# One batch more of ctx and of y transposed by VectorE's 32x32 blocks instead of TensorE, with a few steps put in another order

## The reference, cut to what matters

```python
# x, ctx: (8, 256, 1024); Wq, Wk: (1024, 1024); all float32
text = layernorm(x)
Q = einsum('btx,dx->btd', text, Wq) + bq
K = einsum('bpx,dx->bpd', ctx, Wk) + bk
attn = softmax(einsum('btd,bpd->btp', Q, K) / 32)   # 256 x 256 for each batch
x1 = x + einsum('btp,bpd->btd', attn, ctx)
y = layernorm(x1)
w = 4-bit fields of qweight; wbin = where(w > 0, 1, -1)
weights = scales[g_idx] * (wbin - zeros[g_idx])     # 1024 x 1024
out = x1 + y @ weights + bias
```

## Time and profile before

| | |
|---|---|
| median of 3 runs | 544.64 us |
| the profiled execution's own time | 544.98 us |
| its span, first to last instruction | 543.2 us |
| TensorE busy | 536.7 us, 99% |
| VectorE, ScalarE, GpSimd busy | 367.5, 280.6, 187.2 us |
| granted TensorE clock, mean | 1.000 |
| DRAM traffic | 112.33 MB, mean 207 GB/s |

### The profile page before, as it was taken

The page is one execution under the profiler, slowest core; times in us unless marked ns, Lnnn a source line. Parts: engine busy times, 40 slices in busy tenths (PEclk is TensorE's granted clock), DMA queues, the critical chain, the costliest instruction groups (busy, mean ns, idle before and its releaser), DMA issues.

```text
span 543.2 us, 7422 instructions
## 1 busy us (share of the span) xinstructions
PE 536.7 (99%) x2654; PEld 448.9 (83%) x2654; DVE 367.5 (68%) x600; ACT 280.6 (52%) x496; POOL 187.2 (34%) x151
## 2 busy tenths in 40 slices
PE   8999999999999999999999999999999999999997
PEld 7788788787777877778898999998788888888886
DVE  4988458886888676692415555574768779778742
ACT  5977955314676682333347666686553244325210
POOL 1064000010000000000336877777756744753530
PEclk9999999999999999999999999999999999999999
DMA  8941893459588646845484899998346675773421
GB/s 267 319 157 41 152 158 77 159 148 317 196 250 273 211 162 190 271 97 178 169 282 145 296 357 356 331 414 315 122 139 244 193 248 197 220 233 116 117 78 77
DMA packets 74852, 112.33 MB, mean 207 GB/s; under 512 B 28768, under 2 KB 51368, under 8 KB 72640
## 3 DMA queue, kind: packets, MB, share of 16 engines
q1 hardware_dynamic: 68288, 105.57, 59.0%
q10 hardware_dynamic: 6528, 6.29, 5.6%
HBM read 69.84 MB, written 41.94 MB: 206 GB/s over the span
## 4 chain that ended last, share of the span: by engine, by line
PE 80%; ACT 7%; DVE 5%; DMA 3%; issue 1%; POOL 1%; SPq 1%; ACTq 0%; DVEq 0%; POOLq 0%
PE bank L1364 22%; PE bank L1366 22%; PE bank L1365 22%; PE bank L1402 3%; PE bank L1405 3%; PE bank L1408 3%; PE bank L1454 2%; DMA wk_stage<-in_L_xattn_Wk 1%; DMA xq<-xn_scratch 1%; POOL cn_lo L604 1%; ACT yin L906 1%; DMA right_scratch<-part_hi 1%; ACT xjunk_early L726 1%; DVE xq L1069 1%; ACT wq_bk L681 1%
## 5 line engine op out<-in xcount | busy, mean ns | idle before, releaser
L1364 PE MATMUL bank<-xT_hi,m_hi 128*128 128x512 f32 x256 | 101.0, 395 | 0.0
L1366 PE MATMUL bank<-xT_hi,m_lo 128*128 128x512 f32 x256 | 99.7, 390 | 0.0
L1365 PE MATMUL bank<-xT_lo,m_hi 128*128 128x512 f32 x256 | 99.6, 389 | 0.0
L611 POOL TENSOR_TENSOR tT_lo<-t_pair,tT_hi 128x1024 fp32r<-128x1024 f32 x16 | 38.2, 2402 | 75.5 <-ACT tT_hi L653 75.5
L1316 DVE TENSOR_TENSOR xres<-xres,bank 128x512 f32<-128x512 f32 x56 | 38.2, 682 | 36.2 <-PE bank L1366 36.1
L862 ACT ACTIVATE t_pair<-bank,ucol 128x512 f32<-128x512 f32 x32 | 22.0, 687 | 78.7 <-PE bank L1366 74.1
L625 POOL TENSOR_TENSOR l_lo_s<-l_sum_s,l_hi_s 128x512 fp32r<-128x512 f32 x32 | 40.4, 1293 | 56.0 <-DVE l_sum_s L1257 56.0
L1364 PEld LDWEIGHTS bank<-xT_hi,m_hi 128*128 128x128 f32 x256 | 48.0, 188 | 11.7 <-issue 2.1
L1366 PEld LDWEIGHTS bank<-xT_hi,m_lo 128*128 128x128 f32 x256 | 48.0, 188 | 10.2
L1365 PEld LDWEIGHTS bank<-xT_lo,m_hi 128*128 128x128 f32 x256 | 48.1, 188 | 10.0 <-issue 0.2
L1402 PE MATMUL bank<-wk_hi,wq_hi 128*128 128x512 f32 x128 | 50.4, 394 | 0.4 <-DVE wk_lo L983 0.4
(11 more groups left out here) (158 smaller groups left out, 1245.6 us busy)
## 6 DMA issues: line engine op xcount, KB each, us to landing
xres<-in_x SPq DMA_DIRECT2D x8, 1024.0 KB, 10.0
out<-xres SPq DMA_DIRECT2D x15, 512.0 KB, 5.4
right_scratch<-part_hi SPq DMA_DIRECT2D x28, 256.0 KB, 2.2
cin<-in_ctx SPq DMA_DIRECT2D x7, 1024.0 KB, 6.4
xn_scratch<-xin SPq DMA_DIRECT2D x6, 1024.0 KB, 4.7
xq<-xn_scratch ACTq DMA_DIRECT2D x24, 256.0 KB, 5.4
r_tile<-right_scratch SPq DMA_DIRECT2D x6, 1024.0 KB, 11.4
yn_scratch<-yin SPq DMA_DIRECT2D x6, 1024.0 KB, 4.1
```

The costliest lines, as they stand in the source:

```text
L611: pool.tensor_tensor(tT_lo[b][:, ks, :], t_pair[b // 2][:, b % 2, ks, :], tT_hi[b % 2 if b else 2][:, ks, :].bitcast(F32), ALU.subtract).t ...
L1364: pe.matmul(out_, a_hi, b_hi, start=start, stop=False, skip_group_check=True)
L1365: pe.matmul(out_, a_hi, b_lo, start=False, stop=False, skip_group_check=True)
L1366: return pe.matmul(out_, a_lo, b_hi, start=False, stop=stop, skip_group_check=True)
```

## The change

Parts, with the names in the diff:

- ctx of batch 1 is loaded by quadrants too (`cq[1]`), in place of its load by rows at that point, and transposed by VectorE (`c_blocks(1, u)`), into banks 4 and 5. Its rows come later (`load_ctx(1)`, now four DMAs), after ctx of batch 2.
- TensorE's `c_tr(1, u)` are gone.
- y of batch 1 goes by DRAM: `rows_of_y_by_quadrant(1)` on SP, `y_blocks(1, ...)` on VectorE behind `added(0, 3)`; TensorE's `y_tr(1, ...)` are gone. ScalarE writes `yin` of batch 1 in plain order, and does so ahead of two `left_hi`.
- `gather(6)` follows n = 21 instead of 22.
- On ScalarE, `c_hi(2, 0)` and `c_hi(2, 1)` stand between the two copies to `cn_hi` of batch 0, and `p_hi(7)` stands ahead of `ctx_hi(7)`.
- On VectorE, `residual(6, 0)` stands ahead of `row_max(7)`, and `left_lo(0, "a12")` behind it.
- On SP, the first part of the right factors is loaded after ctx of batch 3 (the fourth) instead of ahead of it.

```diff
@@ -279,10 +282,10 @@
-            return 16 * (b // 3 + 1) + (48 if b % 3 == 0 else 0)
+            return 16 * (b // 3 + 1) + (48 if b % 3 < BLOCKS else 0)
...
         def c_bank(b, u):
-            return bank[(3 if b else 6) + u % 2]
+            return bank[(6, 4, 3)[min(b, 2)] + u % 2]
@@ -306,7 +309,7 @@
-        GATHER = {4: 0, 6: 1, 9: 2, 11: 3, 16: 4, 18: 5, 22: 6, 24: 7}
+        GATHER = {4: 0, 6: 1, 9: 2, 11: 3, 16: 4, 18: 5, 21: 6, 24: 7}
         SUMS = (8, 13, 20, 26)
@@ -405,21 +408,29 @@
-            def load_ctx(b):
+            def load_quadrants_of_ctx(b):
                 if b == 0:
-                    sp.wait_ge(s_cb, 4)
-                elif b == 1:
+                    sp.wait_ge(s_xlo, NB * PAIRS)
+                else:
                     for name in R_SUM:
                         sp.wait_ge(s_lst[name], 16 * KH)
+                pieces = ctx[b].rearrange("(j m) (k a i) -> a j (m k) i", m=NB, a=4, i=32)
+                for a in range(4):
+                    sp.dma_start(cq[b][32 * a:32 * a + 32, :, :].rearrange("p m (k i) -> p (m k) i", i=32),
+                                 pieces[a]).then_inc(s_cql[b], 16)
+
+            def load_ctx(b):
+                if b < BLOCKS:
+                    sp.wait_ge(s_cb, 4 * b + 4)
                 elif b == 2:
...
                     sp.wait_ge(s_cnlo, 4 * (b - 2))
-                    wait(sp, s_ctr, 4 * (b - 3))
-                if b == 0:
-                    rows = ctx[0].rearrange("(j t m) f -> m j t f", t=QT, m=4)
+                    wait(sp, s_ctr, 4 * (b - 4))
+                if b < BLOCKS:
+                    rows = ctx[b].rearrange("(j t m) f -> m j t f", t=QT, m=4)
                     for m in range(4):
-                        sp.dma_start(cin[0][32 * m:32 * m + 32, :, :], rows[m]).then_inc(s_cl[0], 16)
+                        sp.dma_start(cin[b][32 * m:32 * m + 32, :, :], rows[m]).then_inc(s_cl[b], 16)
                 else:
@@ -492,7 +499,7 @@
                         load_raw(b)
-            load_ctx(1)
+            load_quadrants_of_ctx(1)
             load_ctx(0)
@@ -501,8 +508,8 @@
             load_ctx(2)
-            load_right(0, 0, 3)
-            chunks = {0: ((0, 3, 5),), 1: ((0, 5, 7),), 2: ((1, 0, 3),), 3: ((1, 3, 5),), 4: ((1, 5, 7),),
+            load_ctx(1)
+            chunks = {0: ((0, 0, 3),), 1: ((0, 3, 5), (0, 5, 7)), 2: ((1, 0, 3),), 3: ((1, 3, 5),), 4: ((1, 5, 7),),
                       5: ((2, 0, 3),), 6: ((2, 3, 5), (2, 5, 7))}
@@ -526,20 +533,23 @@
+            def rows_of_y_by_quadrant(g):
+                sp.wait_ge(s_yn, QT * (g + 1))
+                sp.dma_start(yn_dram[g].rearrange("(t p) f -> p t f", p=P), yin_of(g)).then_inc(s_ynst, 16)
+                sp.wait_ge(s_ynst, 16 * g)
+                if g == 1:
+                    sp.wait_ge(s_pv, 4 * B)
+                else:
+                    sp.wait_ge(s_yb, 4 * (g - 1))
+                rows = yn_dram[g].rearrange("(m j) f -> j m f", j=32)
+                for a in range(4):
+                    sp.dma_start(yq[32 * a:32 * a + 32, :, :], rows[:, :, a * S:(a + 1) * S]
+                                 ).then_inc(s_yql[g % 2], 16)
+
+            rows_of_y_by_quadrant(1)
             for f in range(B):
-                g = f + 2
-                if g < B:
-                    sp.wait_ge(s_yn, QT * (g + 1))
-                    sp.dma_start(yn_dram[g].rearrange("(t p) f -> p t f", p=P), yin_of(g)).then_inc(s_ynst, 16)
-                    sp.wait_ge(s_ynst, 16 * (g - 1))
-                    if g == 2:
-                        sp.wait_ge(s_pv, 4 * B)
-                    else:
-                        sp.wait_ge(s_yb, 4 * (g - 2))
-                    rows = yn_dram[g].rearrange("(m j) f -> j m f", j=32)
-                    for a in range(4):
-                        sp.dma_start(yq[32 * a:32 * a + 32, :, :], rows[:, :, a * S:(a + 1) * S]
-                                     ).then_inc(s_yql[g % 2], 16)
+                if f + 2 < B:
+                    rows_of_y_by_quadrant(f + 2)
                 for t, n in enumerate((5, 6)):
@@ -814,6 +826,9 @@
                     copy(cn_hi[:, kt, :], cin[b % 3][:, kt, :]).then_inc(s_cnhi, 1)
+                    if b == 0 and kt == 0:
+                        c_hi(2, 0)
+                        c_hi(2, 1)
@@ -925,8 +938,9 @@
                 if b + 1 < B:
-                    c_hi(b + 1, 0)
-                    c_hi(b + 1, 1)
+                    if b != 1:
+                        c_hi(b + 1, 0)
+                        c_hi(b + 1, 1)
                     if b == 1:
@@ -942,13 +956,14 @@
                 exps(b)
+                if b == B - 1:
+                    p_hi(b)
                 ctx_hi(b)
-            p_hi(B - 1)
             act.wait_ge(s_cnlo, 4 * B)
+            y_apply(1, 1)
+            y_apply(1, 0)
             left_hi(0, "s3")
             left_hi(0, "s4")
-            y_apply(1, 1)
-            y_apply(1, 0)
             act.wait_ge(s_pv, 4 * B)
@@ -1161,13 +1176,15 @@
-            def c_blocks(u):
+            def c_blocks(b, u):
                 if u == 0:
-                    dve.wait_ge(s_cql, 64)
+                    dve.wait_ge(s_cql[b], 64)
+                    if b == 1:
+                        dve.wait_ge(s_w, 4 * KH)
                 if u > 1:
-                    dve.wait_ge(s_clo, u - 1)
-                dve.transpose(c_bank(0, u)[:, :].rearrange("p (k m j) -> p m k j", k=2, m=NB),
-                              cq.rearrange("p m (k i) -> p m k i", i=32)[:, :, 2 * u:2 * u + 2, :]).then_inc(s_cb, 1)
+                    dve.wait_ge(s_clo, 4 * b + u - 1)
+                dve.transpose(c_bank(b, u)[:, :].rearrange("p (k m j) -> p m k j", k=2, m=NB),
+                              cq[b].rearrange("p m (k i) -> p m k i", i=32)[:, :, 2 * u:2 * u + 2, :]).then_inc(s_cb, 1)
@@ -1269,8 +1286,11 @@
                 if name == "a21":
-                    dve.wait_ge(s_yql[f % 2], 64 * (f // 2))
+                    dve.wait_ge(s_yql[f % 2], 64 * ((f + 1) // 2))
                     dve.wait_ge(s_lhi, N_PROD * f)
+                    if f == 1:
+                        dve.wait_ge(s_x1, 4 * B)
+                        dve.wait_ge(s_llo_d, 3)
                 dve.transpose(y_bank(f, name)[:, :].rearrange("p (k m j) -> p m k j", k=4, m=4),
@@ -1279,7 +1299,14 @@
                     invert_sum(b - 1)
-                if b + 1 < B:
+                if b == 0:
+                    c_blocks(1, 0)
+                    c_blocks(1, 1)
+                    c_lo(1, 0)
+                    c_blocks(1, 2)
+                    c_lo(1, 1)
+                    c_blocks(1, 3)
+                elif b + 1 < B:
                     c_lo(b + 1, 0)
@@ -1291,10 +1318,16 @@
                     left_lo(0, "a11")
+                    residual(b - 1, 0)
+                row_max(b)
+                if b == B - 1:
                     left_lo(0, "a12")
-                row_max(b)
+                if b == 0:
+                    c_lo(1, 2)
+                    c_lo(1, 3)
                 if b > 0:
-                    residual(b - 1, 0)
+                    if b < B - 1:
+                        residual(b - 1, 0)
                     residual(b - 1, 1)
@@ -1345,6 +1378,9 @@
                 added(f, 3)
+                if f == 0:
+                    for name in ("a21", "a22", "a11", "a12"):
+                        y_blocks(1, name)
                 if f + 1 < B:
@@ -1445,7 +1481,7 @@
                     pe.wait_ge(s_cl[b % 3], ctx_loads(b))
-                if b == 1 and u == 0:
+                if b == BLOCKS and u == 0:
                     pe.wait_ge(s_tev, NB * PAIRS)
@@ -1531,11 +1563,11 @@
                     if j in (3, 7):
-                        if b + 1 < B:
+                        if BLOCKS <= b + 1 < B:
                             c_tr(b + 1, j // 2 - 1)
                             c_tr(b + 1, j // 2)
-                        else:
-                            y_tr(0, ("a21", "a22") if j == 3 else ("a11", "a12"))
+                        elif b + 1 == B:
+                            y_tr(("a21", "a22") if j == 3 else ("a11", "a12"))
@@ -1581,8 +1613,6 @@
                         pv(B - 1)
-                    if b == 0 and n == 3:
-                        y_tr(1, ("a21", "a22", "a11", "a12"))
```

More of the change, by code:

```diff
@@ L26 @@
 N_PROD = len(LEFT)
+BLOCKS = 2
 WARM = 24
@@ L234, in xattn_ffn_kernel @@
         s_cl = [sem(f"ctx_loaded{i}") for i in range(3)]
-        s_cql, s_cb = sem("ctx_by_quadrant_loaded"), sem("ctx_transposed_by_blocks")
+        s_cql = [sem(f"ctx{b}_by_quadrant_loaded") for b in range(BLOCKS)]
+        s_cb = sem("ctx_transposed_by_blocks")
         s_ctr, s_chi, s_clo = sem("ctx_transposed"), sem("cT_hi_done"), sem("cT_lo_done")
```

62 lines of the change are left out of this document (27 added, 35 removed).

## The result

The changed kernel takes 550.95 us (median of 4 runs, 549.92 to 552.65) against 544.71 for the kernel before on the same chip: a ratio of 1.0119, 95% interval 1.0105 to 1.0132. It is slower by 6.2 us. I had forecast slower, 547.3, with a range up to 549.6: the sign and the place were right, the size was not.

The account below looks back on a forecast made before the run. TensorE's own list was taken as the bound (busy 536.7 of 543.2 us). From the median of 544.64: -4.8 gained, +5.8 stall, +1.7 slow clock, sum +2.7, so 547.3 us; range 543.8 to 549.6.

Parts of the forecast that it names:

- What leaves TensorE: Transposes of ctx 1 and batch 1's y, earlier pv(0), and waits removed by new orders: 4.8 us gained together.
- pv(0): In batch 1's attention, pv(0) starts at 291.5, 2.04 us earlier, still bound by the probabilities: 0.28 beside the transposes' 1.76.
- The orders' 0.8 and 0.2: Reordering removes waits at pv(6) and product(0, 1), 0.8 us with restarts, and at gather(7), 0.2 us.
- ctx's blocks covered: VectorE's four ctx 1 transposes are ready before scores(1) needs them, by 0.9 and 0.25 us: no cost.
- Rival D: Stall and slow clock, and ctx's blocks late too by 0.7 to 2 us: 548 to 549.3 us, chance 0.13.
- The stall, 5.8 us: TensorE waits at product(0, 6) for added(0, 4), delayed by batch 1's y through DRAM: 5.8 us, bounds 4.7 to 7.3.
- I take 6.1: Batch 1's y: the four reloads from DRAM take 6.1 us from the first issue, bounds 5.0 and 7.6.
- The clock, 1.7 us: Behind the pause at product(0, 6), matmuls run at the 1.2 GHz level: 1.7 us lost, bounds 0 and twice that.
- rival A: The forecast itself, stall at product(0, 6) and slow clock: 547.3 us, range 545.5 to 549.0, chance 0.5.
- rival B: The stall at product(0, 6), but the clock stays: 545.6 us, or 544.5 with the shortest loads, chance 0.22.
- The rows of ctx 1 and the first right factors come later [...]: nothing.: In SP's queue, these moved loads are needed only some ten and a hundred us afterwards, so they cost nothing.
- Rival C: The DRAM chain for batch 1's y ends in time, no wait at product(0, 6): 539.8 us, chance 0.15.

Follow-up runs that it names:

- version 12: Changed kernel with batch 1's y back on TensorE, the last attention batch's orders turned back and x loaded first: 542.43 us, ratio 0.9959.
- 8: Changed kernel with batch 1's y transposed by TensorE again and the loads of x first: 541.57 us, ratio 0.9946.
- version 6: Changed kernel without the store of batch 1's y, its loads fetching another tensor's rows already in DRAM: 546.23 us, ratio 1.0024.
- version 3: Changed kernel with the first right factors loaded ahead of the rows of ctx 1, as before: 554.38 us, ratio 1.017.
- version 5: Changed kernel with the store of batch 2's y held until batch 1's reload has landed: 552.09 us, ratio 1.0121.
- 2: Changed kernel with 68 identity transposes keeping TensorE at work in the pause ahead of product(0, 6): 547.8 us, ratio 1.0069.
- 11: Changed kernel with the loads of x first and 54 identity transposes filling TensorE's pause: 546.04 us, ratio 1.0039.

## Why the prediction was wrong in size

Right were the list that bounds the kernel, the place and the cause of the stall, and that the clock would fall; the gains were a little larger than forecast. **What failed is one term put at nothing, the moved loads of ctx 1 and of the right factors, and two terms of the right kind but too small, the reload and the clock's price.** With x first and all else as in the change (version 7), the time is 548.17 us, inside the range that I had stated. (Of that difference of 2.8 us the two profiles show 0.8 in the attention, from the loads, and 1.3 in the stall, from the store; the rest shows in no profile.)

- **What leaves TensorE**: 4.8 us forecast, 4.96 measured at the end of product(0, 5). Of it 0.45 come from the head of the program, where the kernels differ by as much from one execution to another, and 0.96 were lost at pv(2). So the gains themselves were larger: 4.96 - 0.45 + 0.96, some 5.5. The part that I had too small is pv(0): between the starts of scores(0) and pv(0) are 13.56 us instead of 16.13, 2.6 less, where I had 2.04. I had put the row maximum behind the fourth block, at 285.1 on the scale of before; it started at 283.36, which is 284.1 on that scale, and the probabilities came earlier with it. The orders' 0.8 and 0.2 were about right (0.7 to 0.9, version 12 against 8).
- **ctx's blocks covered**: right. The timeline of VectorE in the changed kernel, the last of the four blocks and what stands behind it:

```profile
282.72 0.73 DVE L1186 STREAM_TRANSPOSE bank<-cq 128x512 f32<-128x512 f32 x1
283.36 0.65 DVE L1237 TENSOR_REDUCE pairs<-bank 128x2 f32<-128x512 f32 x1
283.93 1.27 DVE L985 TENSOR_TENSOR cT_lo<-bank,cT_hi 128x512 fp32r<-128x512 f32 x2
```

  TensorE has no wait in scores(1), which follows, and none for a `cT_lo` there in any version. Rival D falls.
- **The stall, 5.8 us**: of its terms the store held in most executions (3.99 forecast, 4.05), the four blocks took 3.95 instead of 4.4, and the last piece 2.75 instead of 2.87. **The term that was too small is "I take 6.1" for the loads**: they take 6.8 to 7.1 us in every profile that I followed (7.6 from the other tensor of version 6). The bounds of 5.0 to 7.6 held it. I had let the last one's 6.1 count from the first issue; it is nearer to counting from its own. Together that is a stall of 6.2 us, 0.4 above the forecast. In the profiled execution of the changed kernel, and in that one alone, the store took 5.3, which makes the 7.5: from 388.5 to 390.5 it moved data at 377 to 401 GB/s as in version 7, but its last packets came at 25 to 33 GB/s from 391 to 392. The page's fit, 4.4 us for 1 MB (the Trainium skill, "DMA: Bandwidth & Descriptors", the anatomy of one DMA), is given there for DMAs that GpSimd issues. SP's store of 1 MB is near it with 4.05 us, its reload of 1 MB in four pieces with 7.0 us is not.
- **The clock, 1.7 us**: too small. It is 2.5 to 2.9 behind a pause of 6 us or more (the changed kernel, 3, 5 and 7 against 2 and 11), and 1.7 behind 3.7 (version 6). The bounds that I had set, 0 and twice 1.7, held it; rival A's range took it only to 2. With all of my own bounds (loads 1.5 more, clock 1.7 more) the sum reaches 550.5, so the stated range was narrower than its working. I had taken the loss from the 24 transposes of the start, 4.5 us of work; here the low level held for 5.3 us of it (406.44 to 411.73), with matmuls at 0.43 us instead of 0.23. The rule that I named (the Trainium skill, "TensorE: Matmul & The Clock Gate", Part 1: the throttled state is the default, activity releases it) agrees: rival B falls, and a kernel that keeps TensorE busy doesn't pay (versions 2 and 11, clock 1.00).
- **"The rows of ctx 1 and the first right factors come later [...]: nothing."** **This is the step that was wrong in kind.** I asked when the moved tiles are needed, and not whose load stands behind them in SP's queue, nor whether that load has slack left once the batches start 3 us earlier: x of batch 2 had 0.5 us. It costs 1.0 us in the profile (TensorE at pv(2)), 2.6 in version 3, 3.1 in version 5 with a clock that falls too. The median of the changed kernel fell by 2.8 us when x went first, with the reserve on the store's length told above.

The sum with the terms of the profiled execution: -5.5 + 7.6 + 2.7 + 1.0 = +5.8, less the 0.45 at the head +5.4, as its spans differ by (7.6 is the whole delay of product(0, 6), 7.5 of it the wait). The median has +6.2; there the stall is probably nearer to 6.2 and late x more, which no profile shows. Rival C needed no wait at product(0, 6); even without the store (version 6) added(0, 4) came 3.7 us too late.

What stays open: why x of batch 2 comes 1 us late in one execution and over 3 in another of the same program, and why the store took 5.3 us once. In version 5 SP's issue of the second chunk lasted 1.98 us instead of 0.49, so x was issued 1.5 us later (306.86 instead of 305.40), and it took 16.6 us instead of 15.9; what lengthened both no run here tells.

## What to carry to other kernels

When a transfer is moved or doubled, follow the queue behind it as well as the consumer of the moved tile: the victim is the next load with little slack, and a change that lets the consumers start earlier takes slack from every load by itself. When an operation on the bounding engine is traded for a round trip by DRAM, add up the whole trip (here 2.4 + 4.05 + 7.0 + 4.0 + 2.75 us) against the time until it is needed; 1.75 us of transposes were bought for over 9. And a stall of the tensor engine costs clock behind it: here 1.7 us behind one of 3.7, and 2.5 to 3.0 behind those of 6 to 7.5.
